# Contextual attention: ScalarE copies each score tile out of PSUM first, VectorE takes its maxima from the copy

## The reference, cut to what matters

```python
f  = b[:, :, ::2, ::2]                         # 40 x 40 features
w  = 3x3 patches of f                          # L = 1600 patches of 576 numbers
wn = w / max(norm(w), 1e-4)
yi = einsum('bpd,bld->blp', w, wn)             # scores, 1600 x 1600
yi = softmax(yi * mm * 10, axis=1) * mm        # over l
patches = einsum('blp,bld->bpd', yi, 4x4 patches of b at stride 2)
out = overlap-add of patches at stride 2, cut to 80 x 80, / 4
```

## Time and profile before

| | us |
|---|---|
| median of 3 runs | 1781.02 |
| lowest and highest run | 1776.0 and 1792.49 |
| the profiled execution, own time | 1782.45 |
| its span, first to last instruction | 1780.6 |
| PE busy | 1591.8 (89%) |
| DVE busy | 1090.1 (61%) |
| ACT busy | 901.4 (51%) |
| mean granted TensorE clock | 0.952 of full |

### The profile page before, as it was taken

How to read it: one execution, slowest core, us unless ns; L and a number is a source line. 1 busy time by engine, 2 the same in 40 slices (tenths; PEclk the granted TensorE clock), 3 DMA queues, 4 the chain that set the end, 5 groups by cost and what they waited for, 6 DMA issues and landing times.

```text
span 1780.6 us, 27285 instructions
## 1 busy us (share of the span) xinstructions
PE 1591.8 (89%) x7260; PEld 1052.2 (59%) x7260; DVE 1090.1 (61%) x2526; ACT 901.4 (51%) x2265; POOL 51.2 (3%) x62
## 2 busy tenths in 40 slices
PE   3887899998999899998999989999899989999986
PEld 3756566665666566565665656666566656656543
DVE  5224555675566756576656755667556676667784
ACT  1446454574446744565535645457344573457431
POOL 1000100001000000000000010000100000000100
PEclk9987899999999999998999999999889999999998
DMA  3400624226422445225352262422633234522342
GB/s 61 62 1 12 143 61 89 72 70 139 84 63 72 104 111 106 55 69 124 86 96 61 66 145 66 92 72 73 137 71 77 72 94 109 106 64 66 112 122 78
DMA packets 181701, 149.64 MB, mean 84 GB/s; under 512 B 120016, under 2 KB 177424, under 8 KB 181520
## 3 DMA queue, kind: packets, MB, share of 16 engines
q1 hardware_dynamic: 181522, 147.62, 35.1%
HBM read 19.78 MB, written 13.11 MB: 18 GB/s over the span
## 4 chain that ended last, share of the span: by engine, by line
PE 71%; DVE 10%; ACT 8%; issue 7%; SPq 2%; DMA 1%; DVEq 0%; ACTq 0%; POOL 0%; POOLq 0%
PE psG L433 35%; PE psO L449 30%; DVE S L723 4%; ACT S L575 3%; PE psG L428 3%; DVE G L773 2%; PE psM L347 2%; ACT G L565 2%; ACT OSB L595 1%; ACT G L586 1%; PE psB L362 1%; SPq L251 1%; DVE Z L806 1%; DVE G L784 1%; ACT SQ L529 1%
## 5 line engine op out<-in xcount | busy, mean ns | idle before, releaser
L449 PE MATMUL psO<-Z,B 123*128 123x492 f32 (+2 forms) x1792 | 786.5, 569 | 66.7 <-ACT OSB L595 57.9
L723 DVE CUSTOM_DVE_ANT_0 S<-psG,RB 123x369 f32<-123x369 f32 (+1 forms) x448 | 267.4, 605 | 547.3 <-PE psG L433 471.0
L565 ACT ACTIVATE G<-psG 123x369 f32<-123x369 f32 (+1 forms) x448 | 236.6, 529 | 695.8 <-DVE mx L723 693.9
L449 PEld LDWEIGHTS psO<-Z,B 123*128 123x128 f32 x1792 | 335.9, 199 | 301.3 <-issue 202.3
L433 PE MATMUL psG<-LH,HL 128*123 128x369 f16 (+3 forms) x2592 | 474.8, 329 | 26.2 <-issue 13.8
L433 PEld LDWEIGHTS psG<-LH,HL 128*123 128x123 f16 x2592 | 338.0, 138 | 175.3 <-issue 94.9
L586 ACT ACTIVATE G<-G,nb 123x492 f32<-123x492 f32 (+1 forms) x448 | 268.2, 646 | 125.5 <-DVE G L773 125.1
L575 ACT ACTIVATE S<-S,nm 123x360 f32<-123x360 f32 (+3 forms) x560 | 306.3, 551 | 0.1
L773 DVE SCALAR_TENSOR_TENSOR G<-G,RA,psB 123x492 f32<-123x492 f32 (+1 forms) x448 | 275.4, 658 | 21.8 <-issue 18.2
L784 DVE TENSOR_TENSOR G<-G,SH 123x492 f32<-123x492 f32 (+1 forms) x448 | 251.2, 601 | 14.7 <-DMA SH<-G 14.5
L806 DVE TENSOR_TENSOR Z<-G 123x984 f32<-123x984 f32 (+2 forms) x192 | 209.8, 1093 | 30.4 <-PE psO L449 30.3
(11 more groups left out here) (74 smaller groups left out, 515.2 us busy)
## 6 DMA issues: line engine op xcount, KB each, us to landing
SH<-G SPq DMA_DIRECT2D x224, 214.8 KB
SH<-G SPq DMA_DIRECT2D x224, 161.0 KB
XP<-x SPq DMA_DIRECT2D x20, 280.0 KB, 5.5
XP<-mid SPq DMA_DIRECT2D x20, 280.0 KB, 5.4
SH<-G SPq DMA_DIRECT2D x224, 19.2 KB
HL<-SQ SPq DMA_DIRECT2D x16, 246.5 KB, 3.3
LH<-SQ SPq DMA_DIRECT2D x16, 246.5 KB, 4.5
SH<-G SPq DMA_DIRECT2D x224, 14.4 KB
```

The costliest lines, as they stand in the source:

```text
L449: last = pe.matmul(psO[:, b, 0:n], B[:, o:o + 128], Z[:, 2 * (s % 2) + j, 0:n], start=t == 0, stop=t == TILES - 1)
L565: act.activation(G[:, t * GLEN + c0:t * GLEN + c0 + n], psG[0:TW, par, 0:n], ACT.Copy).then_inc(g_read, 1)
L723: dve.tensor_tensor_reduce(S[:, par, 0:n], psG[0:TW, par, 0:n], RB[:, s0 * TW:s0 * TW + n], 1.0, 0.0, ALU.mult, ALU.max, mx[:, par:par + 1 ...
```

## The change

- ACT copies each score tile from `psG` to `G` as soon as PE has made it. The copy no longer waits for the maximum, but waits itself for what it may overwrite in `G` (`columns_free`, the same waits as before). Two semaphores, one for each bank, replace `g_read`.
- DVE takes its product and maximum from `G` and waits for the copy. `S` and `mx` have four places in place of two.
- ACT takes the exponentials and sums of a pair one pair later. The order in its slot is now: read-out, copy of `par` 0, softmax, copy of `par` 1, sums of the pair before, the rest.
- In slots 16 and 21 PE makes the tiles in another order: one, paste, two, paste, one.
- `psM` shrinks to one bank; two of the four scale rows use the banks of `psB`. The last scale row moves from slot 4 to 18, the scales of the next unit on DVE from slot 13 to 20, the first log-sum row on PE from the middle of slot 24 to its end.
- In the log-sum, the sum of the last chunk's two parts moves from `lse_max` to `lse_sum`, which now waits for the later sums.

```diff
+        ROW_BANK = [psB[0:TW, 1, :], psB[0:TW, 1, :], psM[0:TW, :], psB[0:TW, 0, :]]
...
             def scale_rows(u, v, g):
 
                 pe.wait_ge(r_step, (v + 1) * R_STEPS)
-                if g == 0 and u is not None:
+                if u is not None:
                     pe.sem_inc(pe_gate, 1)
-                    pe.wait_ge(b_made, u * PAIRS + 4)
-                if g == 2 and u is not None:
+                    if g == 2:
+                        pe.wait_ge(b_made, (u + 1) * PAIRS)
+                    else:
+                        pe.wait_ge(arg_made, u * NB + (3 if g == 3 else NK) * TILES)
+                if g == 1:
                     pe.sem_inc(pe_gate, 1)
...
-                spread(psM[0:TW, ROW_BANK[g], :], R, 4 * g, min(4 * g + 4, TILES)).then_inc(r_psum, 1)
-
-            def lse_row(v, k):
+                    pe.wait_ge(r_rows, v * 4 + 1)
+                spread(ROW_BANK[g], R, 4 * g, min(4 * g + 4, TILES)).then_inc(r_psum, 1)
...
+            def lse_row(v, w, k):
 
                 pe.wait_ge(lse_dve, v * LSE_STEPS + (LSE_STEPS // 2 if k == 0 else LSE_STEPS))
-                if k >= 2:
-                    pe.sem_inc(pe_gate, 1)
+                pe.sem_inc(pe_gate, 1)
+                if k == 0:
+                    pe.wait_ge(r_rows, v * 4 + 4)
+                elif k == 1 and w is not None:
+                    pe.wait_ge(r_rows, w * 4 + 2)
+                else:
                     pe.wait_ge(arg_made, v * NB + (k - 1) * TILES)
-                elif not (isinstance(v, int) and v == 0):
-                    pe.sem_inc(pe_gate, 1)
-                    pe.wait_ge(arg_made, (v - 1) * NB + (k + 3) * TILES)
                 s0, n = P_CHUNKS[k]
                 spread(psB[0:TW, k % 2, :], lse, s0, s0 + n).then_inc(lse_rows, 1)
...
             def score_tile(v, j, par):
-                k, t = j // PAIRS, 2 * (j % PAIRS) + par
-                s0, w = S_CHUNKS[k]
-                at = v * NB + 2 * j + par
-
-                stored_n = w if t < s0 else max(0, t // 2 * 2 - s0) if t < s0 + w else 0
-                if stored_n and par == 0:
-                    pe.wait_ge(g_read, at + FREE)
-                else:
-                    pe.wait_ge(g_read, at + 1)
-                for i in range(stored_n):
+                s0 = S_CHUNKS[j // PAIRS][0]
+                t = 2 * (j % PAIRS) + par
+                w, stored = tile_blocks(j, par)
+                pe.wait_ge((even_read, odd_read)[par], v * SLOTS + j + 1)
+                if stored and par == 0:
+
+                    pe.sem_inc(pe_gate, 1)
+                    pe.wait_ge(odd_read, v * SLOTS + j + 1)
...
                     pairs = score_list(s) if v is not None else []
                     if s == 4 and v is not None:
                         scale_rows(u, v, 2)
+                    if s == 18 and v is not None:
                         scale_rows(u, v, 3)
...
-                    tiles = [(p, par) for p in pairs for par in range(2)]
-                    for j in range(2):
-                        for p, par in tiles[len(pairs) * j:len(pairs) * (j + 1)]:
-                            score_tile(v, p, par)
-                        if s == 24 and j == 0 and v is not None:
-                            lse_row(v, 0)
-                        if at:
-                            paste_tile(at, s, j)
+                    if pairs:
+                        score_tile(v, pairs[0], 0)
+                    if at:
+                        paste_tile(at, s, 0)
+                    if pairs:
+                        score_tile(v, pairs[0], 1)
+                    if len(pairs) == 2:
+                        score_tile(v, pairs[1], 0)
+                    if at:
+                        paste_tile(at, s, 1)
+                    if len(pairs) == 2:
+                        score_tile(v, pairs[1], 1)
+                    if s == 24 and v is not None:
+                        lse_row(v, w, 0)
...
                     if w is not None and s in (25, 26):
-                        scale_rows(v, w, s - 25)
+                        scale_rows(u, w, s - 25)
                 if v is not None:
-                    lse_row(v, 1)
+                    lse_row(v, w, 1)
...
-                act.activation(B[:, g * 512:(g + 1) * 512], psM[0:TW, BLOCK_BANK[g], :], ACT.Copy).then_inc(b_made, 1)
-
-            def score_pair(u, v, j):
+                act.activation(B[:, g * 512:(g + 1) * 512], psM[0:TW, :], ACT.Copy).then_inc(b_made, 1)
+
+            def columns_free(u, j, par):
+
                 k, i = j // PAIRS, j % PAIRS
+                if u is not None:
+                    if k == 0:
+                        act.wait_ge(wrap_made, u * PAIRS + min(i + 2, PAIRS))
+                        act.sem_inc(act_gate, 1)
+                    act.wait_ge(z_made, u * SLOTS + k * PAIRS + min(i + par + 1, PAIRS) + 1)
+                    act.sem_inc(act_gate, 1)
+
+            def copy_scores(u, v, j, par):
+                k, t = j // PAIRS, 2 * (j % PAIRS) + par
                 s0, w = S_CHUNKS[k]
-                c0, n = (s0 + 1) * TW, w * TW
-                if k == 0 and u is not None:
-                    act.wait_ge(wrap_made, u * PAIRS + min(i + 2, PAIRS))
-                    act.sem_inc(act_gate, 1)
-                for par in range(FREE):
-                    t = 2 * i + par
-                    if u is not None:
-
-                        act.wait_ge(z_made, u * SLOTS + k * PAIRS + min(i + par + 1, PAIRS) + 1)
-                        act.sem_inc(act_gate, 1)
-                    act.wait_ge(max_made, v * NB + 2 * j + par + 1)
-                    act.activation(G[:, t * GLEN + c0:t * GLEN + c0 + n], psG[0:TW, par, 0:n], ACT.Copy).then_inc(g_read, 1)
+                columns_free(u, j, par)
+                act.wait_ge(g_ready, v * NB + 2 * j + par + 1)
+                c = t * GLEN + (s0 + 1) * TW
+                act.activation(G[:, c:c + w * TW], psG[0:TW, par, 0:w * TW],
+                               ACT.Copy).then_inc((even_read, odd_read)[par], 1)
+
+            def score_sums(v, j):
+                k, i = j // PAIRS, j % PAIRS
+                n = S_CHUNKS[k][1] * TW
                 act.wait_ge(neg_made, v * SLOTS + j + 1)
                 for par in range(FREE):
                     t = 2 * i + par
-                    e = S[:, par, 0:n].rearrange("p (s w) -> p s w", w=PITCH)
+                    e = S[:, 2 * (j % 2) + par, 0:n].rearrange("p (s w) -> p s w", w=PITCH)
                     parts = [e[:, :, 0:HALF]]
                     if k == NK - 1:
                         parts = [e[:, 0:8, 0:HALF], e[:, 9:11, 0:HALF]]
...
                     at = place(u, v, s + LEAD)
-                    if s == 24 and v is not None:
-                        lse_log(v, False)
-                    elif at:
-                        softmax_pair(at)
+                    pairs = score_list(s) if v is not None else []
                     if u is not None and s % PAIRS == 0 and s <= SLOTS:
                         read_out(u, s // PAIRS - 1)
-                    if s == 23 and v is not None:
-                        lse_exp(v, False)
+                    for n, j in enumerate(pairs):
+                        copy_scores(u, v, j, 0)
+                        if at and n == 0 and s != 24:
+                            softmax_pair(at)
+                        copy_scores(u, v, j, 1)
+                        if s == 23:
+                            lse_exp(v, False)
+                        if s == 24:
+                            lse_log(v, False)
+                        if j:
+                            score_sums(v, j - 1)
+                    if s == SLOTS and v is not None:
+                        score_sums(v, SLOTS - 1)
+                    if at and not pairs:
+                        softmax_pair(at)
                     if s == SLOTS and v is not None:
                         lse_exp(v, True)
                     if s == SLOTS + 1 and v is not None:
                         lse_log(v, True)
-                    if v is not None:
-                        for j in score_list(s):
-                            score_pair(u, v, j)
                     if s == 24 and at:
                         softmax_pair(at)
                     if s == 4 and v is not None:
                         scale_rows(v, 2)
+                    if s == 18 and v is not None:
                         scale_rows(v, 3)
...
-                if i == 0 and k in (0, 2):
-                    dve.wait_ge(r_rows, v * 4 + k + 2)
+                if i == 0 and k != 1:
+                    dve.wait_ge(r_rows, v * 4 + max(k + 1, 2))
                     dve.sem_inc(dve_gate, 1)
-                for par in range(FREE):
+                slot = 2 * (j % 2)
+                for par, read in enumerate((even_read, odd_read)):
+                    c = (2 * i + par) * GLEN + (s0 + 1) * TW
                     dve.wait_ge(s_read, v * NB + 2 * j + par + 1)
                     dve.sem_inc(dve_gate, 1)
```

(29 more changed lines are left out.)

71 lines of the change are left out of this document (33 added, 38 removed).

## The result

The changed kernel takes 1721.25 us (median of 4, 1719.51 to 1724.65) against 1784.18 (median of 4, 1776.0 to 1792.49) for the kernel before: ratio 0.9649, 95% interval 0.9599 to 0.97. The forecast was 1711, from 1676 to 1762. The profiled execution took 1719.51 with a span of 1717.7, 1.8 around it; before it was 1782.45 with 1780.6. So 62.9 us of span have to be found.

The account below looks back on a forecast made before the run. The prediction took PE as the bound. Gains of 8.1 us a body over seven full bodies (57), 9 in the first and 5 in the last sum to 71, giving 1711 us, range 1676 to 1762.

Parts of the forecast that it names:

- the read-out's place: Read-out at the head of slots 7, 14 and 28: PE's waits for it shrink by 4.4 us a body.
- transposed waits: PE's waits for ACT's copy of transposed score tiles: one handover in place of two, 0.9 us a body gained.
- the new pair order: PE's tile order in slots 16 and 21: an unhidden copy and hand-over costs 0.7 us in each.
- the log-sum: Log-sum rows, sums a slot later: waits of 1.2 us, then 0.7, in place of 2.3; net gain 0.4 a body.
- the jump back: Loop's jump back, 2.8 us a body; next unit's features would bind there only after 4.8 us regained, so don't.
- Clock: PE's clock after shorter waits: 2.4 us a body gained, 1.6 behind slot 7 and 0.8 behind the log-sum wait.
- First and last body: First body gains 9 us (0 to 15) from shorter handovers; last gains 5 (2 to 7) from earlier read-outs.
- rival B: Nothing moves: the read-out gain returns as waits for `Z` or the features; 1781 us, chance 0.14.
- Rival A: Only read-outs gain; new handovers lose in slots where ACT has no idle time: 4.0 us a body, 1750 us, chance 0.16.
- Rival C: Slower: PE waits on a loop of odd copy, maxima, argument and softmax in transposed slots; 1818 us, chance 0.08.
- Costed at nothing: Later maxima, moved scales on DVE, one bank of `psM`, SBUF maximum and wrap copies: taken as zero in the sum.
- the worst case: GpSimd's seven wrap copies a body each meeting one DVE maximum: at most 4.7 us a body, taken as nothing.

Follow-up runs that it names:

- before_readout_head: The kernel before, with only the read-out moved ahead of the softmax pair of its slot: 1730.39 us, ratio 0.9696.
- max_first: The changed kernel with DVE's maximum read from `psG` again, the copy waiting for it, and slot 24's logarithm ahead of both copies: 1803.03 us, ratio 1.0102.
- before_copy_first: The kernel before with the read-out at the slot's head and the early copy, maximum from `G`, sums in their own slot: 1785.53 us, ratio 0.9974.
- old_pair_order: The changed kernel with PE's old order in slots 16 and 21 (two tiles, paste, two tiles, paste): 1691.14 us, ratio 0.9477.
- lse_early: The changed kernel with slot 24's logarithm ahead of the odd copy on ACT and the log-sum columns ahead of `Z` on DVE: 1700.62 us, ratio 0.9523.
- few_features: The changed kernel without four of each unit's eight feature DMAs (those to `H1` and `HV`), leaving out part of the computation: 1695.13 us, ratio 0.9481.
- late_readout: The changed kernel with the read-out behind the softmax pair of its slot again: 1808.29 us, ratio 1.014.
- own_sums: The changed kernel with each pair's sums taken in that pair's own slot again: 1759.98 us, ratio 0.9865.

## Why the prediction was right, and where its terms were off

**Right: PE is the bound, and the read-out's place is the main term.** The prediction took 4.4 us a body out of the waits; 4.9 went (7.7 to 2.8). Slot 14 has none, as said. Slot 7 waits 0.96 where 1.3 was forecast, slot 28 1.86 where it was 2. before_readout_head shows that the place alone takes out 3.3 of the 4.9 and gives 54 of the 63 us in time. The prediction had up to 0.7 from the earlier copy in each of slots 7 and 28; no run takes apart whether the other 1.6 come from the copy or from the later sums.

**Right: transposed waits.** 3.2 became 2.1, 1.1 gained for 0.9. With the old pair order they are 0.7 a body (3.6 over five). max_first and before_copy_first show that it takes the early copy and the later sums: without the first 9.2 a body, in the old order without the second 5.0.

**Mis-sized: the new pair order.** It was charged with 0.7 in slots 16 and 21, 1.4 us a body. The waits are 1.3 a body (6.7 over five), so the term for waiting was right. But old_pair_order is 30 us faster, since 6.4 us of clock in five bodies and 9 us in the head came with it, and neither was charged. Which matmuls of the head got faster wasn't traced.

**Wrong in sign: the log-sum.** Forecast was a gain of 0.4, with 1.2 in slot 24 and 0.7 at the end. Measured are 2.07 and 0.86, a loss of 0.6 a body. The second row was right. In slot 24 I counted only DVE's wait for the sums and left out the queue on ACT. All engines around it:

```profile
561.63 0.18 DVE L783 TENSOR_REDUCE tot<-df 123x4 f32<-123x16 f32 x1
562.67 1.09 DVE L833 TENSOR_TENSOR Z<-G 123x902 f32<-123x902 f32 x1
563.94 0.58 ACT L574 ACTIVATE G<-psG 123x492 f32<-123x492 f32 x1 [2.12 <-DVE Z L833]
564.42 0.20 ACT L626 ACTIVATE lns<-tot 123x4 f32<-123x4 f32 x1
564.85 0.16 DVE L790 TENSOR_TENSOR lse<-tot,big 123x4 f32<-123x4 f32 x1
565.29 0.85 PE L364 MATMUL psB<-idn,lse 123*123 123x123 f32 x4 [2.07 <-DVE lse L790]
```

`tot` is ready at 561.8. The logarithm starts at 564.42, because the copy ahead of it in ACT's queue waits 2.12 for `Z` to free its columns. lse_early takes it out from behind that copy, and `lse` on DVE out from behind `Z`, and the wait goes; the two weren't run apart.

**Not foreseen: the jump back.** Its 2.8 grew to 3.7, and 5.7 over five bodies (13.8 to 19.5). The prediction named the features as the thing that might bind there, and excluded it rightly; few_features shows it. The room shrank, though: PE goes on 2.0 behind the last landing (603.42 against 601.4), where in the kernel before it was 5.6 (842.9 against 831.4 + 5.9 = 837.3; the prediction's 838.4 counts the landing from the end of the issue). What holds PE there wasn't found. Over five bodies the wait is 12.1 in late_readout, 13.8 in the kernel before, 14.0 to 14.8 in before_copy_first, before_readout_head and own_sums, 18.1 to 21.2 in the changed kernel and the versions that are faster than it, and 22.7 in max_first, so it goes neither with the length of a body nor with one of the edits. No run varied it by itself.

**Clock: right in size by luck.** The forecast was 2.4 a body, slot 7's 1.6 and half of the log-sum's, with slot 28's 2.6 kept. Measured are 11.1 / 5 = 2.2, but in other places. Slot 7's loss was there in only three of the five bodies of the kernel before (3.40, 3.48 and 3.65, otherwise 1.92) and is in none now: 4.8 in five bodies, 1.0 each. Slot 28's 16 pastes took 45.4 in five bodies (8.54 to 9.90 each) and take 36.0 now (8.56 once, then 6.87): 1.9 each, which the forecast had kept out. At the jump back the nine score matmuls took 1.62 in three of five bodies and 2.91 and 3.03 in the others; now they take about 3.03 in all five, which loses 0.9 each. So the step that failed here is reading one body's row as the price in every body. That before_readout_head gets 4.0 a body from the clock, from fewer edits, shows that the other edits together give some of it back; 1.3 of that is the pair order's.

**First and last body.** 9 was forecast for the first; the first read-out, in slot 7 of the body behind it, comes 16.6 earlier, 11.8 of it in the waits (20.0 to 8.2), where the term took 9; max_first shows that they are the early copy's. The clock there rose from 0.86 to 0.91, which the prediction had counted only in the far end of its range, 15. The last body was put at 5. From the last full body's read-out to the last read-out there are 106.6 us against 108.9, 2.3 gained. In standing still 5.0 went (14.6 to 9.6), as forecast, and the matmuls took 2.5 more. PE lost the waits for the read-out and met more waits for `Z`, which the prediction had named only in rival B.

**The sum.** 33 in five bodies is 6.6 a body, forecast 8.1. The shortfall of 10 over seven bodies comes from the log-sum (1.0) and the jump back (0.9), and is part made good by the first body. Rival A, that only the read-outs gain, holds for the full bodies on the net: 1026 against 1024 with the read-out alone. It named as cause a loss at each new handover in slots where ACT has no idle time; what the runs show is the pair order (15 in five bodies) and the log-sum (8), and a longer jump back (5.7). With the old pair order the early copy and the later sums gain 13 in five bodies, against A. Its price of 4.0 a body was too small all the same, since the read-out alone brought 7. Rival C isn't in the changed kernel, and max_first is what it looks like.

**Costed at nothing.** The maximum from SBUF takes 669 ns against 668 for 492 columns, and 549 against 541 for 369. By the cycle table of the Trainium skill (VectorE: DVE Perf Modes, "The TRN2 errata") it would have been an estimated 65 ns shorter; the measurement decides, and it is no shorter. The wrap copies take 944 ns on average, 828 before: they lose 116 ns each, 0.8 us a body, on a mostly idle engine. With the Trainium skill (SBUF — State Buffer, "SBUF: two separate sides") the trace agrees in direction, and the losing side is GpSimd, at a sixth of the worst case that the prediction had set aside. The one bank of `psM` shows in the first body alone: PE waits there 2.1 us in 3 for ACT to copy an image block before it makes the next, a wait that the kernel before doesn't have.

## What to carry to other kernels

On an engine that works its queue in order, put first what another engine waits for: here a read-out of 1.1 us ahead of a softmax gave 3.0%, and a logarithm of 0.2 us ahead of a copy, with its columns ahead of `Z` on DVE, gave 1.2%. An early handover pays only if nothing in the same queue still waits for the late one (the early copy alone lost about 50 us against the same kernel without it, together with the later sums and in the old order on PE it gained 39). When a reorder moves several things at once, try each back alone: the change was worth 63 us, and 30 more lay in one of its own parts.
